# A steady batch's third projection part split over two slots, one normalisation and one low part a slot later

## The reference

```
q, k, v = x Wq^T, x Wk^T, x Wv^T          16 heads of 16 features, rotary on q and k
attn    = softmax(q k^T / 4, causal) v     per head
x1      = layernorm(x + attn Wo^T)
h       = silu(x1 w_gate) * (x1 w_up)      1024 features; of each 4 the 2 largest by size are kept
out     = layernorm(x1 + h w_down)
```

## Time and profile before

| what | us |
|---|---|
| median of 3 runs | 729.64 |
| lowest and highest run | 729.32, 729.65 |
| profiled execution, its time | 727.83 |
| profiled execution, its span | 726.1 |
| mean granted clock of TensorE | 0.974 |

### The profile page before, as it was taken

The page is one execution under the profiler, slowest core; times in us unless marked ns, Lnnn a source line. Parts: engine busy times, 40 slices in busy tenths (PEclk is TensorE's granted clock), DMA queues, the critical chain, the costliest instruction groups (busy, mean ns, idle before and its releaser), DMA issues. The chain is left out here.

```text
span 726.1 us, 13794 instructions
## 1 busy us (share of the span) xinstructions
PE 665.6 (92%) x5264; PEld 492.8 (68%) x5264; DVE 561.0 (77%) x825; ACT 407.6 (56%) x578; POOL 320.0 (44%) x317
## 2 busy tenths in 40 slices
PE   7979788999999999998989988989999999999984
PEld 6655554657565565655645656788989898989883
DVE  5888656778777787877787376878897989898976
ACT  5551566576867768666576764535453535363522
POOL 4485876677867778532233133024040312213030
PEclk9997899999999999999999999989999999999997
DMA  4048646355464554558111102112111102010101
GB/s 127 29 107 164 156 111 188 115 149 159 135 180 146 150 168 125 155 155 285 39 59 34 59 1 78 40 45 72 59 36 51 58 29 81 5 58 0 59 1 58
DMA packets 48815, 67.61 MB, mean 93 GB/s; under 512 B 6456, under 2 KB 27448, under 8 KB 48760
## 3 DMA queue, kind: packets, MB, share of 16 engines
q1 hardware_dynamic: 47860, 65.23, 31.1%
q10 hardware_dynamic: 900, 1.64, 0.9%
HBM read 43.12 MB, written 23.07 MB: 91 GB/s over the span
## 5 line engine op out<-in xcount | busy, mean ns | idle before, releaser
L941 DVE TENSOR_REDUCE bmax<-mx_ps 128x8 f32<-128x1024 f32 (+1 forms) x148 | 180.8, 1222 | 80.8 <-PE mx_ps L1219 79.9
L782 ACT ACTIVATE prob<-ex_ps 128x1024 f32<-128x1024 f32 x160 | 163.9, 1024 | 84.6 <-PE ex_ps L1249 80.3
L612 POOL TENSOR_SCALAR_AFFINE_SELECT prob<-prob 128x512 f32<-128x512 f32 x128 | 88.2, 704 | 128.3 <-ACT prob L782 128.3
L1266 PE MATMUL pv_ps<-prob,v_sb 128*32 128x512 f32 (+3 forms) x1024 | 83.1, 443 | 2.0 <-POOL prob L612 2.0
L1204 PEld LDWEIGHTS mx_ps<-mask_b,half_id 64*128 64x128 bf16 x592 | 16.9, 94 | 80.3 <-DVE bmax L941 68.8
L1204 PE MATMUL mx_ps<-mask_b,half_id 64*128 64x128 bf16 x592 | 46.0, 234 | 24.6 <-DVE bmax L941 21.9
L1507 POOL TENSOR_TENSOR hm_l<-v_sb,hm_h 128x2048 fp32r<-128x2048 f32 x4 | 18.5, 4622 | 90.4 <-ACT hm_h L1568 90.4
L1507 POOL TENSOR_TENSOR k_st<-v_sb,q_st 128x2048 fp32r<-128x2048 f32 x3 | 13.9, 4626 | 75.6 <-ACT q_st L1568 75.6
L1266 PEld LDWEIGHTS pv_ps<-prob,v_sb 128*32 128x32 f32 x1024 | 25.7, 110 | 28.9 <-issue 24.8
L1554 ACT ACTIVATE g_sb<-ex_ps 128x512 f32<-128x512 f32 x28 | 16.6, 591 | 45.7 <-PE ex_ps L1770 45.7
L1816 PE MATMUL mi_ps<-wd_h,q_st 128*128 128x256 f32 x128 | 37.7, 294 | 3.4 <-DVE k_st L1686 3.4
(11 more groups left out here) (261 smaller groups left out, 1987.2 us busy)
## 6 DMA issues: line engine op xcount, KB each, us to landing
y_sb<-x SPq DMA_DIRECT2D x12, 512.0 KB, 3.9
xT_sb<-xT SPq DMA_DIRECT2D x8, 512.0 KB, 4.4
q_st<-q_parts SPq DMA_DIRECT2D x32, 128.0 KB, 2.8
k_st<-k_parts SPq DMA_DIRECT2D x32, 128.0 KB, 3.0
x<-y_sb SPq DMA_DIRECT2D x8, 512.0 KB, 3.3
xh<-x SPq DMA_DIRECT2D x8, 512.0 KB, 3.9
q_parts<-qk_rot SPq DMA_DIRECT2D x14, 256.0 KB, 3.1
k_parts<-qk_rot SPq DMA_DIRECT2D x14, 256.0 KB, 2.8
```

Source lines behind the costliest of these rows:

```text
L612: nc.gpsimd.affine_select(out=block, in_=block, compare_op=ALU.is_ge, fill=0.0, base=0, pattern=[[0, n], [1, P]], channel_multiplier=-1).t ...
L782: nc.scalar.activation(out, ex_ps[:], ACT.Exp).then_inc(ex_act, 1)
L941: nc.vector.tensor_reduce(out=out, in_=src, axis=AX.X, op=ALU.max).then_inc(mx_read, 1)
L1266: last = nc.tensor.matmul(pv_ps[32 * g:32 * g + 32, P * kt:], v_sb[b % 2][:, kt, G4 * j + g, :], probs(g), start=kt == 0, stop=kt == 2, sk ...
```

## The change

The third projection part (QK 2) of batches 3 to 7 is made in two halves: the three products of c = 0 stay in slot 14, the three of c = 1 come in slot 15 ahead of the other entries of that slot, into the same bank. ScalarE's copy of the part moves from slot 14 to slot 15, ahead of the copy of the maxima. The low part 0 of those batches moves on VectorE from slot 14 to slot 15, and with it its two spill transfers on SyncE's queue from slot 15 to slot 16, past the `fill_stack` of slot 15. The normalisation of the head outputs of tokens 256 to 383 (O 2) of all batches moves from slot 6 to slot 7. Nothing is added to or taken from the computation.

```diff
-HIGH_AT, LOW_AT = [-47, -45, -40, -39], [-46, -44, -38, -37]
+HIGH_AT, LOW_AT = [-47, -45, -40, -39], [-45, -44, -38, -37]
+
+QK_REST, QK_REST_AT = 2, -45
...
@@ scalar
+                if (b := batch_at(g, QK_REST_AT)) is not None and b > 2:
+                    ev_qk(b, QK_REST)
                 for op, b, i in misc_at(g):
-                    if op == "QK":
+                    if op == "QK" and b > 2 and i == QK_REST:
+                        continue
+                    elif op == "QK":
                         ev_qk(b, i)
...
@@ vector
                 for t in range(NT):
-                    for b in batches_of(g, "O", t, later=1):
+                    for b in batches_of(g, "O", t, later=2 if t == 2 else 1):
                         normalise(b, t)
...
@@ tensor
-            def three_terms(out, lh, ll, rh, rl):
-                terms = [(a, r, c) for c in range(NC) for a, r in ((lh, rh), (lh, rl), (ll, rh))]
-                for n, (a, r, c) in enumerate(terms):
-                    last = nc.tensor.matmul(out, a(c), r(c), start=n == 0, stop=n == len(terms) - 1)
+            def three_terms(out, lh, ll, rh, rl, cs=range(NC)):
+                terms = [(a, r, c, n) for c in cs for n, (a, r) in enumerate(((lh, rh), (lh, rl), (ll, rh)))]
+                for a, r, c, n in terms:
+                    last = nc.tensor.matmul(out, a(c), r(c), start=c == 0 and n == 0, stop=c == NC - 1 and n == 2)
                 return last
 
-            def project_qk(b, t):
-                out = start_bank("QK", b, t)
+            def in_halves(b, t):
+                return b > 2 and t == QK_REST
+
+            def project_qk(b, t, rest=False):
+                out = mi_ps[USES["QK", b, t][0]] if rest else start_bank("QK", b, t)
...
-                    three_terms(out[:], lambda c: wqkv_h[:, c, features], lambda c: wqkv_l[:, c, features],
-                                lambda c: xh[par][:, c, :], lambda c: xl[par][:, c, :]).then_inc(made("QK", b, t), 1)
+                    cs = range(NC) if not in_halves(b, t) else range(1, NC) if rest else range(1)
+                    last = three_terms(out[:], lambda c: wqkv_h[:, c, features], lambda c: wqkv_l[:, c, features],
+                                       lambda c: xh[par][:, c, :], lambda c: xl[par][:, c, :], cs)
+                    if rest or not in_halves(b, t):
+                        last.then_inc(made("QK", b, t), 1)
...
+                if (b := batch_at(g, QK_REST_AT)) is not None and in_halves(b, QK_REST):
+                    project_qk(b, QK_REST, rest=True)
                 for op, b, i in misc_at(g):
                     other(op, b, i)
```

## The result

The changed kernel takes **725.08 us** (median of 11 runs, 722.13 to 728.60) against 729.64 (727.42 to 729.99, 11 runs beside it): ratio 0.9944, 95% interval 0.9926 to 0.9961. Two repeats, on two chips, gave smaller gains: ratios 0.9968 [0.9951, 0.9984] and 0.9962 [0.9939, 0.9986]. In the means the three gains are 4.06, 2.27 and 3.26 us, 3.2 on average, each with 1 to 1.4 us of uncertainty to either side. The profiled execution is one of the best, 722.13 us (span 720.4) against 727.83.

A forecast was written before the change was run, and what follows sets the result against it. Each slot was taken to end on the later of TensorE's own work and VectorE's maximum; 0.68 + 0.26 + 1.3 = 2.24 us less took the median from 729.64 to 727.4 us, range 726.0 to 729.0.

The forecast's parts named there:

- the bound of 2.19: Slot 15's upper bound, if the switch after the projection costs as much again as the first matmul's extra 0.10 us.
- the term 4 x (0.06 + 0.11) = 0.68: Slots 14 and 15, projections of batches 4 to 7: 0.06 and 0.11 us less each, 0.68 us in all.
- The term of the seventh period: Later normalisation in the seventh period, beside weight casts: 0.25 to 0.35 us less, taken as 0.3.
- The 0.25 us of idle time: VectorE's only idle time before the maximum of slot 8 in the seventh period, limiting the later normalisation's gain there.
- The 0.26 us of the first batch: Projection of batch 3: slot 14 gains 0.45 us, slot 15 loses 0.19, net 0.26 less.
- the floor of 1.90: Slot 15's length in us as set by VectorE's maximum alone, read from the batch without projections.
- my own 2.09: Slot 15's forecast length in us, TensorE-bound: 0.74 + 0.34 + 0.24 + 0.24 + 0.53.
- its price of 1.7 us a time: Cost of one stretch mostly at 1.2 GHz, from the 3.85 us slot at the turn to the second period.
- a low stretch that falls away: One way to gain more than forecast, beside slot 15 at its floor: 725.7 to 726.5 us; chance 0.10.
- The clock rival: TensorE's clock falls after idle in slot 14: one stretch 729.1 us, two 730.8; chance 0.08 (0.06 slower, 0.02 one stretch).
- The bound of 0.2%: What a measurement of this kernel was said to tell from no change: about 0.2%, 1.46 us.

The follow-up runs named there:

- The change again: The changed kernel, unaltered, measured twice more against the kernel before: 726.16 against 728.64 us, and on another chip 725.89 against 729.64 us.

## Why the prediction was right and wrong

**The slots: right in mechanism, the sum right partly by luck.** Outside the seventh period every length after the change came out within 0.02 us for slots 14, 15, 7 and 8, the matmul order of slot 15 was that of the prologue, the bound of 2.19 wasn't needed, and VectorE's two low parts of slot 13, in front of the maximum, do set slot 14 at 2.33. The moves on SyncE, ScalarE and GpSimd cost nothing. But the term 4 x (0.06 + 0.11) = 0.68 is too small: the four batches gave 0.85, because slot 15 was 2.23, 2.22 and 2.23 before in the three whose rows I didn't take, and only 2.20 in the one I did, and slot 14 gave 0.07. That this and the next term, too large, nearly cancel (2.23 against 2.24) is luck. The gain was carried on: from the last masks to the first feed-forward matmul it is 76.93 us before and 76.92 after.

**The term of the seventh period: wrong in size.** I took 0.3 and measured 0.08, in the sum of slots 7 to 10. Slot 7 gave 0.60, but slots 8 and 9 took 0.29 each. VectorE of the changed kernel there, and of before:

```profile
358.50 1.22 DVE L947 TENSOR_REDUCE bmax<-mx_ps 128x8 f32<-128x1024 f32 x1
...
360.26 0.98 DVE L1016 CAST w_up_parts<-qk_rot 128x512 fp32r<-128x512 f32 x1
361.15 1.22 DVE L947 TENSOR_REDUCE bmax<-mx_ps 128x8 f32<-128x1024 f32 x1
```

```profile
364.69 0.68 DVE L1010 CAST w_up_parts<-qk_rot 128x512 fp32r<-128x512 f32 x1
...
366.41 0.91 DVE L1010 CAST w_up_parts<-qk_rot 128x512 fp32r<-128x512 f32 x1
```

The 0.25 us of idle time was used up as forecast, but I costed the cast behind it at the length that it had: it grew from 0.68 to 0.98. Of the eight casts of this kind in each profile, one takes 0.90 to 1.01 us (0.78 in one profile) and the others 0.60 to 0.70. Before, the long one (0.91) stood behind slot 9's maximum; now it stands in front of it. The long ones lie beside GpSimd's causal masks, but so does the one of 0.68 in before; why isn't settled.

**The credit for the projection's part: wrong.** The 0.26 us of the first batch came out and the 0.68 of the four became 0.85, but I read slot 15's gain as one of both edits. The low part alone gives 0.30 to 0.33 there, and the halves give 0.11 back in four batches of five. I had the rows for it: the floor of 1.90 beside my own 2.09 said that TensorE would hold slot 15 only because of the halves.

**The step that failed**: "Sum: 0.68 + 0.26 + 1.3 = 2.24 us, 0.31%. The profiled execution's 727.83 becomes 725.6, and the median 729.64 becomes 727.4 us". It moves a difference in slots straight to the median, as if everything beside the slots cost the same in both measurements. What the runs showed in its place: the slots gave their 2.23, and on top of it came what differs between measurements of one kernel, 0 to 1.8 us in the means of three. Part of that is the clock. The versions spend 32 to 47 us at half clock, and the change 0.7 us less than before in one group and 6.2 less in another, worth 0.2 and 1.5 us at 0.24 each. I had the mechanism, with its price of 1.7 us a time, mostly as a rival that takes away; "a low stretch that falls away" stood within a case of 0.10, at 725.7, and the range ended at 726.0, short of even one. With two such stretches fewer, as the first profile of the change has them, it would have reached to about 724 (727.4 - 2 x 1.7).

**The clock rival: wrong in place.** Nothing fell in the steady batches: the changed kernel stands at 1.00 from 118.8 to the feed-forward phase in its first profile and from 126.1 on in the repeats, slots with 0.6 us idle included. The Trainium skill ("TensorE: Matmul & The Clock Gate", "A second HAM failure mode") says that frequent small idles between groups of matmuls make the clock oscillate. The steady slots don't bear it out, with 0.57 us of idle at the end of slot 14 at full clock; the two thin slots in a row do, in some executions.

**The bound of 0.2%** was too fine. Runs of the kernel before spread over 725.2 to 734.8 us in the later groups, and even 12 against 34 runs leave an interval of 0.15% or more on either side. Not all of this spread is the clock's. TensorE's first projection product started between 10.19 and 12.20 us in the 17 profiles, ahead of every low stretch in them, and the loop's first masks between 72.05 and 73.94 us, though the changed kernel's instructions are those of before up to 108 us. In two of these profiles the step ahead of that product (line 677 of ScalarE) had waited 2.8 and 4.2 us for an input's transfer, and the product started at 10.75 and 12.20.

**Open**: how much of the first 4.56 us was the clock's. The changed kernel had 0.9738 there, 38.0 us at half clock, 4 to 6 less than the kernel before in the other groups. At 0.24 us each this makes 0.9 to 1.4 of the 1.8 us that are left in the mean (4.06 - 2.2), and the rest is within the measurement's uncertainty of about 1 us; but the clocks of before's runs in that group aren't known, so this isn't shown. Open too are what, beside the clock and the first transfers, makes runs of one kernel differ, and why the normalisation alone makes the clock fall more often.

## What to carry to other kernels

Count a change to a schedule in stage lengths at full clock, and show these apart from the time: they can be forecast to 0.02 us where no neighbour changes its length, and held against each other they show at once which edit of a bundle works. Where the page shows stretches at a lower clock, the median holds a second term that may fall either way; put it into the range on both sides, with the price of one stretch from the trace, and judge by repeats and by more than one profile. An equal mean clock alone isn't enough: three profiles of the changed kernel, all at 0.979, have spans of 720.4, 723.4 and 723.4 us. And before splitting a step over two slots, work out each slot's floor on every engine: a half moved into a slot that another engine had just left shorter lengthens it.

## What was unexpected of the hardware

TensorE's clock isn't decided by what the kernel does alone. In the first profile of the changed kernel two slots with 0.87 of 1.96 and 0.81 of 1.90 us busy were followed by one of 2.28 us at 2.4 GHz:

```profile
116.84:118.80 1.96, 0.87 (x14) 1.00 0.08 16
118.80:120.70 1.90, 0.81 (x10) 1.00 0.69 205
120.70:122.98 2.28, 2.28 (x34) 1.00 0.91 191
```

In the last repeat the same kernel, busy for the same 0.87 and 0.81 us in the same two slots, went on with one of 3.88 us, mostly at 1.2 GHz (the rows under "The change again").

And a kernel whose slots are 1.1 us shorter in sum can take longer: the normalisation alone, 730.60 against 728.64 us, with a mean clock of 0.9685 against 0.9713.
